# Relative-position attention on one core: the two key blocks' maxima joined in SBUF, and one product with the unit matrix a query group in place of two

## The reference, cut to what matters

```
qk = einsum('bhld,bhrd->bhlr', q, k) / sqrt(16) + einsum('bhld,lrd->bhlr', q, rel)
att = softmax(qk, axis=-1)
out = einsum('bhlr,bhrd->bhld', att, v)
```

## Time and profile before

| | |
|---|---|
| median of three runs | 5952.92 us |
| the profiled execution's own time | 5973.55 us |
| its span | 5971.8 us |
| granted TensorE clock, mean | 0.994 |
| PE / PEld busy | 97% / 90% |
| DVE busy | 82% |
| ACT / POOL busy | 51% / 56% |
| DMA queues, largest share of 16 engines' span | 37.8% |

### The profile page before, as it was taken

How to read it: one execution, slowest core, us unless ns; L and a number is a source line. 1 busy time by engine, 2 the same in 40 slices (tenths; PEclk the granted TensorE clock), 3 DMA queues, 4 the chain that set the end, 5 groups by cost and what they waited for, 6 DMA issues and landing times.

```text
span 5971.8 us, 378300 instructions
## 1 busy us (share of the span) xinstructions
PE 5815.1 (97%) x161792; PEld 5385.6 (90%) x161792; DVE 4903.6 (82%) x10178; ACT 3069.3 (51%) x5160; POOL 3328.2 (56%) x5182
## 2 busy tenths in 40 slices
PE   6999999999999999999999999999999999999997
PEld 5999999999999999999999899999999999999996
DVE  5888888888888888888888888888888888888886
ACT  3555555555555555555555555555555555555554
POOL 4555555555555555555555555555555555555555
PEclk8999999999999999999999999999999999999998
DMA  5343343443434334343343434334344343433432
GB/s 152 85 102 94 91 116 85 106 102 86 113 91 115 88 87 114 93 110 90 92 110 90 112 94 100 95 90 117 83 107 100 89 110 90 116 87 88 113 95 53
DMA packets 1461087, 589.65 MB, mean 99 GB/s; under 512 B 1127168, under 2 KB 1425136, under 8 KB 1459376
## 3 DMA queue, kind: packets, MB, share of 16 engines
q1 hardware_dynamic: 1454752, 562.48, 37.8%
q10 hardware_dynamic: 4624, 2.60, 0.2%
HBM read 476.43 MB, written 89.85 MB: 95 GB/s over the span
## 4 chain that ended last, share of the span: by engine, by line
PE 83%; DVE 10%; issue 3%; DVEq 2%; POOL 1%; SPq 0%; POOLq 0%; DMA 0%; ACT 0%
PE sc L730 21%; PE pw L757 15%; PE sc L747 15%; PE sc L724 14%; DVE r L1185 5%; PE pm L778 4%; PE pw L778 4%; PE pm L738 4%; PE pw L764 3%; DVE xn L1099 2%; DVE nmm L1197 1%; DVEq L1196 1%; DVE y2n L1099 1%; PE pm L797 1%; DVEq L1095 1%
## 5 line engine op out<-in xcount | busy, mean ns | idle before, releaser
L1185 DVE TRANSPOSE_TENSOR_REDUCE r<-sc 128x32 f16<-128x1024 f32 x2048 | 2542.9, 1242 | 22.3 <-PE sc L730 19.0
L1018 ACT ACTIVATE prob<-sc 128x1024 f32<-128x1024 f32 x2048 | 2098.8, 1025 | 213.9 <-PE sc L747 176.9
L730 PE MATMUL sc<-rm,tw 128*128 128x48 f16 (+1 forms) x49152 | 2144.6, 194 | 11.6 <-issue 11.4
L730 PEld LDWEIGHTS sc<-rm,tw 128*128 128x128 f16 x49152 | 1754.4, 100 | 13.6 <-issue 13.2
L724 PE MATMUL sc<-qm,ks 96*128 96x64 f16 x32768 | 1635.8, 193 | 23.2 <-POOL rm L592 13.8
L747 PE MATMUL sc<-nmm,pick 128*128 128x64 f16 x32768 | 1297.5, 193 | 40.5 <-DVE nmm L1197 32.1
L724 PEld LDWEIGHTS sc<-qm,ks 96*128 96x128 f16 x32768 | 1298.3, 98 | 35.2 <-issue 21.9
L1194 DVE TENSOR_REDUCE nm<-pm 16x32 f16<-16x256 f32 x2048 | 834.8, 408 | 557.5 <-PE pm L738 540.9
L747 PEld LDWEIGHTS sc<-nmm,pick 128*128 128x128 f16 x32768 | 1128.7, 98 | 179.2 <-DVE nmm L1197 91.3
L757 PE MATMUL pw<-prob,vs 128*32 128x128 f32 x32768 | 1117.9, 276 | 12.5 <-issue 8.1
L757 PEld LDWEIGHTS pw<-prob,vs 128*32 128x32 f32 x32768 | 840.1, 109 | 76.0 <-issue 14.6
(11 more groups left out here) (153 smaller groups left out, 5766.2 us busy)
## 6 DMA issues: line engine op xcount, KB each, us to landing
raw<-qk_s SPq DMA_DIRECT2D x3096, 64.0 KB, 2.9
tw<-tw_s SPq DMA_DIRECT2D x512, 288.0 KB, 4.0
v_s<-vpad SPq DMA_DIRECT2D x136, 256.0 KB, 3.4
vs<-v_s SPq DMA_DIRECT2D x64, 512.0 KB, 4.4
qm<-qk_s SPq DMA_DIRECT2D x768, 32.0 KB, 2.1
ks<-qk_s SPq DMA_DIRECT2D x378, 64.0 KB, 3.4
qk_s<-qkh SPq DMA_DIRECT2D x272, 64.0 KB, 2.9
qk_s<-qkl SPq DMA_DIRECT2D x272, 64.0 KB, 2.6
```

The lines of the kernel that those rows point to most:

```text
L730: last = mm(out3[:, :, OCT * m + q:OCT * m + q + n], tw[:, s, jp, u:u + P], rm[:, i, m, r * H:(r + n) * H].rearrange("p (h e) -> p h e", e=n),
L1018: A(prob[:, jp % 2, :, :, i * IW:(i + 1) * IW], sc[:, 2 * buf:2 * buf + 2, :].rearrange("p c (h i) -> p c h i", i=IW), ACT.Exp).then_inc(s ...
L1185: v.tensor_reduce(r1[:, 0:2 * H], sc[:, 2 * buf:2 * buf + 2, :].rearrange("p c (h i) -> p (c h) i", i=IW), axis=AX.X, op=ALU.max, apply_tr ...
```

## The change

Behind `maxima`'s reduction, DVE drains and then takes, in a second reduction, the larger of the two key blocks' values for each of the 16 heads: `r2[:, 0:16]` from `r1` as 16 x 2. The semaphore `s_rmax` is now signalled by this second reduction. `transpose_max` makes one product from `r2` (128 x 128, of which the columns behind the first 16 are zeros) in place of two from `r1`. `p_max` has 128 columns in place of 256, so that line 1194 reads 16 x 128 in place of 16 x 256 and joins four values in place of eight.

```
-        r1 = sb("r1", [P, H + P], f16)
+        r1 = sb("r1", [P, 2, H], f16)
+        r2 = sb("r2", [P, P], f16)
...
-        p_max = pm[:, 0:2 * P]
+        p_max = pm[:, 0:P]
...
-            g.memset(r1[:, :], 0.0)
+            g.memset(r2[:, :], 0.0)
...
             def transpose_max(g_count):
                 pe.wait_ge(s_rmax, g_count)
-                for c in range(2):
-                    last = mm(p_max[:, c * P:(c + 1) * P], r1[:, c * H:c * H + P], ident16[:, :], start=True, stop=True)
-                last.then_inc(s_maxT, 1)
+                mm(p_max, r2[:, :], ident16[:, :], start=True, stop=True).then_inc(s_maxT, 1)
...
                 dve.wait_ge(s_scores, count)
-                v.tensor_reduce(r1[:, 0:2 * H], sc[:, 2 * buf:2 * buf + 2, :].rearrange("p c (h i) -> p (c h) i", i=IW),
-                                axis=AX.X, op=ALU.max, apply_transpose=True).then_inc(s_rmax, 1)
+                v.tensor_reduce(r1[:, :, :].rearrange("p c h -> p (c h)"),
+                                sc[:, 2 * buf:2 * buf + 2, :].rearrange("p c (h i) -> p (c h) i", i=IW),
+                                axis=AX.X, op=ALU.max, apply_transpose=True)
+                dve.drain()
+                v.tensor_reduce(r2[:, 0:H], r1[:, :, :].rearrange("p c h -> p h c"), axis=AX.X,
+                                op=ALU.max).then_inc(s_rmax, 1)
```

## The result

The changed kernel takes 6157.48 us, the median of four runs (6155.98 to 6162.84), beside 5954.99 us before: a ratio of 1.0341, 95% interval 1.0323 to 1.0359, +202 us. The forecast was 6022 us, +69 us, with a range of 5970 to 6120. The direction was right, the size was not: most of the loss comes from a collision that no term of the sum holds.

The account below looks back on a forecast made before the run. PE was taken to pace ten of sixteen intervals, DVE six. Terms -550 + 334 + 297 + 55 + 400 = +536 ns a tile, x 128 tiles = +69 us, gave 6022 us from the 5952.92 median; range 5970 to 6120.

Parts of the forecast that it names:

- rival D: Second reduction on DVE as cheap as the shortest row, 92 ns: -18 us, 5935 us; chance 0.02.
- the term for 4 to 5: Group 4 to 5: line 1197 is held until POOL's `wp` is done, so the whole delay counts, +297 ns.
- 7 to 8 and 8 to 9: Two intervals paced by DVE, `side` ahead of line 1194: 2 x (297 - 130) = +334 ns.
- 15 to 0: Interval paced by DVE, `y2n` ahead of line 1194: delay of two groups comes in, +445 ns before the masks.
- 0 to 1: Interval paced by DVE, `y2n` ahead of line 1194 in group 0: +167 ns before the masks.
- the masks: POOL's masks hold DVE in groups 15 to 1: +130 ns if line 1197 gets ahead, +660 if not; 400 taken.
- 5 to 6 and 6 to 7: 5 to 6 paced by PE, one product less, -55 ns; 6 to 7, line 1197 held by POOL's `qkl`, +55 ns.
- The sign "0.05 us behind the new reduction in at least the six intervals": Expected in the profile after: line 738's load follows the new reduction by 0.05 us in the six DVE-paced intervals.
- 12 to 13: One of ten intervals paced by PE: one product less, -55 ns.
- A: Line 1197 of group 5 arrives behind POOL's `qkb` and waits for all of it: +83 us, 6105 us; chance 0.30.
- B: Cost hidden: reduction only 159 ns and line 1197 ahead of the mask, +5 us, 5958 us; chance 0.07.
- C: Groups 14 to 0: DVE's collisions with POOL's masks fall away, -66 us, 5887 us; chance 0.08.

Follow-up runs that it names:

- b_g3_extra: Kernel before, with a drain and one more reduction (result unused) behind the maxima of group 3 alone: 6148.07 us, ratio 1.0316.
- b_g3_drain: Kernel before, with a drain alone, no reduction, behind the maxima of group 3: 6143.57 us, ratio 1.0312.
- b_g3_three_small: Kernel before, with three small reductions of a constant, no drain, behind the maxima of group 3: 6147.99 us, ratio 1.0311.
- a_g3_old: Changed kernel, with group 3's maxima done the old way (no second reduction, two products, 256 columns read): 5970.5 us, ratio 1.0024.
- b_g3_two_small: Kernel before, with two small reductions of a constant, no drain, behind the maxima of group 3: 5982.86 us, ratio 1.0038.

## Why the prediction was wrong, point by point

**The reading of the kernel before** held: PE paces most intervals, DVE six of them (in the trace before, the load of line 738 stands 0.05 us behind the maxima in six and 0.34 us or more in ten). So did the prices: 55 ns for the product (shown by making it twice), 274 ns for line 1194 (278), and 187 + 74 = 261 ns for the reduction and the drain in front of it (297; 0.07 us from the end of line 1184 at 4038.36 to the start of 1188 at 4038.43). The profile after agrees with the Trainium skill, "VectorE: DVE Perf Modes", section on the TRN2 errata, in its fixed term of about 150 cycles: an estimate from it is 190 ns for 32 elements, and 187 were measured. Its table's 94 ns, near which rival D's 92 lay, is out.

**The step that failed** is the term for 4 to 5: "a sooner line 1194 buys nothing: +297". It took line 1197 as the only instruction of DVE in that interval that meets `wp`, and so the 0.297 us delay as the most that could come in; for `side` behind the maxima it said the same, "where `side` makes it late it is up to 297". But the `side` work of group 3, `xn`, stands ahead of line 1194 of group 4 and had its own neighbour: `wp`, only 0.22 us behind it, less than the forecast's own 0.297. Moved by 0.31 us against `wp`, `xn` was held for all of it, and line 1197 then met POOL's next sum. The spare had been counted only to the next load of line 738, and `xn` of group 3 looked safe because in the trace before it was never held. Interval 4 cost +1739 in place of +297 ns; the difference, 1442 x 128 = 185 us, is more than the whole miss of 135 us. b_g3_extra, b_g3_drain and b_g3_three_small put it into the old kernel (+185 to +192 us), a_g3_old takes it out of the new one (6157 to 5970), and there interval 4 stands at +248, close to the +297.

**The other terms.** The two clean ones paced by DVE, 7 to 8 and 8 to 9, came to +248 for +334, mostly the 2 x 36 of the cheaper reduction. 15 to 0 was right, +418 for +445. 0 to 1 was wrong in sign, -358 for +167: line 1200 of group 0 takes 0.18 us in place of 0.56, so of the two outcomes that the forecast gave for the masks (+130 and +660 for both intervals) the good one came, and more: +60. 5 to 6 and 6 to 7 came to +157 and -148 for -55 and +55, with line 1200 of group 5 held by POOL's `qkh`, 0.76 us here, so that 5 to 6 was the one of the ten that DVE came to pace. The sign "0.05 us behind the new reduction in at least the six intervals" came in five of the six: the loads of groups 0, 1, 5, 8 and 9, and now 6, stand 0.05 us behind it, that of 7 stands 0.36 us behind. Line 1200 of group 5 as it was held:

```profile
4044.17 1.04 POOL L606 TENSOR_TENSOR qkh<-qkb,one 128x512 f16<-128x512 f32 x1 [0.21 <-issue]
4044.50 0.76 DVE L1200 TENSOR_TENSOR nmm<-nm,mask_h 16x64 f16<-16x64 f16 x1
```

12 to 13 fell by 142 in place of 55, in the changed kernel and in every variant of it (86 with the product made twice). The other 87 come from a wait of PE that the sum left out. Before, line 1194 of group 12 ends at 4041.17, and PE's next small product into the same bank, for which `maxima_read` waits, is loaded at 4041.22, behind the loads of the scores that end at 4041.19:

```profile
4040.76 0.41 DVE L1194 TENSOR_REDUCE nm<-pm 16x32 f16<-16x256 f32 x1 [1.03 <-PE pm L738]
4040.76 0.43 PEld L730 LDWEIGHTS sc<-rm,tw 128*128 128x128 f16 x12
```

After, the same line (1197) is through before the scores are, and the product is loaded with no wait, 0.08 us ahead of the end of their loads:

```profile
4064.25 0.28 DVE L1197 TENSOR_REDUCE nm<-pm 16x32 f16<-16x128 f32 x1 [0.73 <-PE pm L738]
4064.26 0.43 PEld L731 LDWEIGHTS sc<-rm,tw 128*128 128x128 f16 x12
...
4064.61 0.57 PEld L777 LDWEIGHTS pm<-w_base,x1T 128*128 128x128 f16 x6
```

In the median, PE's load stands 0.05 us behind the end of that line before, as it does behind every reduction that it waits for, and 0.09 us behind it after. So a sooner end of line 1194 also pays in one interval that PE paces.

**The rivals.** A was the right kind of case at the wrong place: an instruction of DVE that loses its turn to one of POOL. It was given 0.3 for group 5 by a margin of 20 ns; group 3, with a margin of 220 against the forecast's own 297, was a near certainty that was not looked at. B and D need a sum near zero and are out. C, the collisions with the masks falling away, came true in part (0 to 1) and was outweighed.

**Without the collision** the forecast of +69 us would also have been too high: a_g3_old is at +14. What the medians say there: the PE-paced intervals -749 ns for the -550 taken (5 to 6 alone -163), the masks +53 for +400, against +248 at 4 to 5, +158 at 6 to 7 and +262 at 7 to 9. Their sum, -28, is -4 us, and the two traces differ by as much (5966.6 and 5971.8 us); the +14 compares medians of runs, and the profiled execution of the kernel before lay 19 us above its median. That lands near rival B (+5), by other terms.

## What to carry to other kernels

A delay added to an engine has two things to pass: the consumer of its result, and, for every instruction behind it, whatever instruction of another engine can hold it. List each instruction of DVE with a long one of POOL that starts shortly behind it; such a pair costs nothing in the trace before, and here it cost nearly a whole POOL instruction (1.7 of 2.04 us) once the order turned. Where a change pays in some stages and costs in others, unrolled code lets each stage have its own version: that turned +3.4% into -1.6%, of which, by the means, about half was the saving that had been worked out.

## What was not expected of the hardware

**The edge is sharp and lies ahead of the start.** With `xn` recorded 0.11 us or more ahead of `wp` it gets through in all 123 such tiles (b_g3_two_small), with 0.04 to 0.08 us ahead it is held in all 120 (b_g3_three_small). The Trainium skill, "SBUF — State Buffer", practical consequences, says that `tensor_scalar` in a two-port mode and a GpSimd instruction exclude each other for the whole instruction, and that the issue order decides. The traces agree with the whole instruction (2.04 to 2.24 us held, `wp` 2.04); but a recorded start 0.05 us ahead is not yet first, so the recorded starts give the order only beyond about 0.1 us.

**A drain can cost more than its gap.** `xn` starts 0.08 us ahead of the end of the maxima without a drain, and 0.23 us behind it with one (b_g3_drain), though the profile shows nothing that it waited for. With the reduction in between (the changed kernel) `xn` starts 0.01 us ahead of the reduction's end. So from the end of the maxima the drain alone moved `xn` by 0.31 us, nearly as much as the drain and the reduction together (0.33 us in the changed kernel, 0.35 in b_g3_extra). Why stays open; that `xn`'s own waits, already satisfied, are only taken up after the drain is a guess.
